# Two transformer layers with cross-attention: the first norm ahead of the context work, the last store in four parts, and a first score with another wait

## The reference

```
x = x + attention(layer_norm(x), layer_norm(x))     # 16 heads of 64, 1024 keys
x = x + attention(layer_norm(x), context)           # 16 heads of 64, 77 keys
x = x + (a * gelu(gate)) @ w2 + b2                  # a, gate = split(layer_norm(x) @ w1 + b1), 1024 wide
```

## Time and profile before

| | us |
|---|---|
| median of 3 runs | 2322.5 |
| lowest and highest | 2322.38, 2325.73 |
| profiled execution, its own time | 2328.06 |
| its span, first to last instruction | 2326.3 |
| TensorE busy | 2142.8 (92%) |
| VectorE busy | 1743.6 (75%) |
| ScalarE busy | 1476.1 (63%) |
| GpSimd busy | 1155.2 (50%) |
| mean granted TensorE clock | 0.990 |

### The profile page before, as it was taken

How to read it: one execution, slowest core, us unless ns; L and a number is a source line. 1 busy time by engine, 2 the same in 40 slices (tenths; PEclk the granted TensorE clock), 3 DMA queues, 4 the chain that set the end, 5 groups by cost and what they waited for, 6 DMA issues and landing times.

```text
span 2326.3 us, 59157 instructions
## 1 busy us (share of the span) xinstructions
PE 2142.8 (92%) x25392; PEld 1434.0 (62%) x25392; DVE 1743.6 (75%) x3148; ACT 1476.1 (63%) x1948; POOL 1155.2 (50%) x730
## 2 busy tenths in 40 slices
PE   4999999999899999989989999998998999999899
PEld 1566666675556666667556666666755666667675
DVE  5888888557588888755768888866576888886664
ACT  2788788345388888823547887773353888786342
POOL 3666665233076766622326766652223667664231
PEclk8999999999999999999999999999999999999999
DMA  3222221000132222001032222100103223210000
GB/s 107 71 73 52 61 62 38 10 31 23 51 105 52 58 74 63 18 10 38 24 83 73 52 75 77 43 27 1 38 23 81 70 61 83 61 36 20 10 11 19
DMA packets 60165, 114.19 MB, mean 49 GB/s; under 512 B 9344, under 2 KB 21632, under 8 KB 59904
## 3 DMA queue, kind: packets, MB, share of 16 engines
q1 hardware_dynamic: 59904, 110.41, 17.5%
HBM read 55.72 MB, written 4.19 MB: 26 GB/s over the span
## 4 chain that ended last, share of the span: by engine, by line
PE 65%; DVE 21%; ACT 9%; issue 3%; DMA 1%; POOL 1%; SPq 0%; POOLq 0%; DVEq 0%; ACTq 0%
PE scores L861 7%; DVE minima L1411 7%; PE scores L854 7%; PE work L831 7%; PE scores L746 6%; PE scores L748 6%; PE scores L747 6%; DVE prob L1426 4%; PE work L746 4%; PE work L747 4%; PE work L748 4%; PE work L883 3%; PE work L879 3%; PE work L881 3%; ACT prob L1214 3%
## 5 line engine op out<-in xcount | busy, mean ns | idle before, releaser
L693 POOL TENSOR_TENSOR prob<-prob 128x1024 f16<-128x1024 f32 x256 | 584.7, 2284 | 556.0 <-ACT prob L1215 545.2
L1411 DVE TENSOR_REDUCE minima<-work 128x1 f32<-128x512 f32 x1024 | 680.2, 684 | 43.0 <-PE work L831 29.4
L1214 ACT ACTIVATE prob<-scores 128x1024 f32<-128x1024 f32 x512 | 525.6, 1026 | 129.2 <-PE scores L861 112.0
L1215 ACT ACTIVATE prob<-scores 128x1024 f16<-128x1024 f32 x512 | 523.3, 1022 | 0.0
L883 PE MATMUL work<-vals,prob 128*128 128x65 f16 x4096 | 429.6, 196 | 0.0
L881 PE MATMUL work<-vals,prob 128*128 128x64 f16 x4096 | 429.4, 193 | 0.0
L879 PE MATMUL work<-vals,prob 128*128 128x65 f16 x4096 | 429.0, 193 | 0.4
L879 PEld LDWEIGHTS work<-vals,prob 128*128 128x128 f16 x4096 | 383.1, 99 | 62.1 <-issue 3.1
L881 PEld LDWEIGHTS work<-vals,prob 128*128 128x128 f16 x4096 | 379.9, 97 | 58.2
L831 PE MATMUL work<-ka,qa 128*128 128x512 f16 x1024 | 390.5, 386 | 24.0 <-DVE minima L1411 18.2
L883 PEld LDWEIGHTS work<-vals,prob 128*128 128x128 f16 x4096 | 380.3, 97 | 0.0
(11 more groups left out here) (160 smaller groups left out, 4179.0 us busy)
## 6 DMA issues: line engine op xcount, KB each, us to landing
qa<-staged_q SPq DMA_DIRECT2D x128, 128.0 KB, 2.3
ka<-staged_k SPq DMA_DIRECT2D x128, 128.0 KB, 2.3
raw_even<-in_pairs SPq DMA_DIRECT2D x32, 384.0 KB, 3.3
raw_odd<-in_pairs SPq DMA_DIRECT2D x32, 384.0 KB, 3.3
raw_odd<-in_pieces SPq DMA_DIRECT2D x20, 512.0 KB, 3.7
raw_even<-in_pieces SPq DMA_DIRECT2D x20, 512.0 KB, 3.6
qb<-staged_q SPq DMA_DIRECT2D x64, 128.0 KB, 2.3
kb<-staged_k SPq DMA_DIRECT2D x64, 128.0 KB, 2.3
```

Source lines behind the costliest of these rows:

```text
L693: pool.tensor_tensor(prob[1][:, slot, :], prob32[:, slot, :], prob[0][:, slot, :], ALU.subtract).then_inc(a.polished, 1)
L1214: act.activation(prob32[:, n % RING, :], source, ACT.Exp)
L1215: act.activation(prob[0][:, n % RING, :], source, ACT.Exp)\
L1411: dve.tensor_reduce(minima[:, t, h:h + 1], out[:, :], AX.X, ALU.max, negate=True)\
```

## The change

The first norm and the six first projections now stand ahead of all work on the context, the ones and the weights on each engine. GpSimd computes its four rstd pairs before it splits the two weight pairs. VectorE sets its first ones and zeros, waits for the constants and starts the norm; the rest of its setting, the context's subtraction and the mask stand behind the mark "v1". ScalarE copies the context behind "v1", and TensorE waits for ones and context there. The context is loaded into `o_nat` in place of `t32`, which the norm uses. The last round's x is stored in four parts, each when its two tiles are done. The first score of a round waits for the round's first six projections alone, not for the seventh.

```diff
--- before.py
+++ after.py
@@ -407,7 +407,7 @@
         x_rows = qa[0]
         spread32 = prob32[:, 0, 0:X_HALF]
         mask_full = prob32[:, 1, 0:len(X_PARTS)]
-        c32 = t32[:, :, :, :].rearrange("p a b c -> p (a b c)")[:, 0:BATCH * 2 * CTX_COLS]
+        c32 = o_nat[:, :, :, :].rearrange("p a b c -> p (a b c)")[:, 0:BATCH * 2 * CTX_COLS]
 
         def o_part(s, t):
 
@@ -588,8 +588,13 @@
                     if (g + 1) % BATCH == 0:
                         sp.wait_ge(bias_added, (g + 1) * 3 + CREDIT)
                         load_rows((g + 1) // BATCH)
-            store(ROUNDS - 1)
-            sp.wait_ge(x_stored, ROUNDS * 16 + CREDIT)
+            for p in range(GROUPS):
+
+                sp.wait_ge(y_free, (ROUNDS * 3 - 1) * TILES + 2 * (p + 1) + 2)
+                tiles = slice(2 * p, 2 * (p + 1))
+                sp.dma_start(io["out"][(ROUNDS - 1) % BATCH, 2 * p * P:2 * (p + 1) * P, :]
+                             .rearrange("(t p) d -> p t d", p=P), x[:, tiles, :]).then_inc(x_stored, 16)
+            sp.wait_ge(x_stored, (ROUNDS - 1 + GROUPS) * 16 + CREDIT)
 
         @block.gpsimd
         def _(pool):
@@ -715,11 +720,11 @@
                     elif n == 6:
                         split_piece(9)
 
-            split_pair("S")
-            split_pair("C")
             pool.sem_inc(bias_added, CREDIT)
             for p in range(GROUPS):
                 norm(0, p)
+            split_pair("S")
+            split_pair("C")
             for g in range(ROUNDS):
                 attention(g)
                 for p in range(GROUPS):
@@ -840,7 +845,7 @@
                     elif step.kind == "score":
                         if pace.here("score") == 0:
 
-                            pe.wait_ge(a.work_free, pace.n(*HIGH) + HIGH_RING)
+                            pe.wait_ge(a.work_free, g * HIGHS + len(first_high) + HIGH_RING)
                         elif pace.here("score") == 1 and g:
 
                             pe.wait_ge(y_free, g * (3 * TILES) + 2)
@@ -1139,11 +1144,12 @@
                             ahead(name)
 
             pe.wait_ge(consts_ready, 10 + 2 * len(X_PARTS))
-            pe.wait_ge(ones_ready, 2)
-            hold(pe, ctx_split, 1)
             for p in range(GROUPS):
                 turn(0, p)
             walk = attention(0)
+            walk("v1")
+            pe.wait_ge(ones_ready, 2)
+            hold(pe, ctx_split, 1)
             for g in range(ROUNDS):
                 cross(g, walk)
                 walk = attention(g + 1) if g + 1 < ROUNDS else None
@@ -1296,17 +1302,18 @@
                     norm(index + 1, 2)
                     norm(index + 1, 3)
 
-            act.wait_ge(ctx_loaded, 16)
+            act.wait_ge(consts_ready, 10 + 2 * len(X_PARTS))
+            act.wait_ge(params_loaded, 16)
+            for p in range(GROUPS):
+                norm(0, p)
+            walk = attention(0)
+            walk("v1")
+            hold(act, ctx_loaded, 16)
             for b in range(BATCH):
                 for part in range(2):
                     cols = slice((2 * b + part) * CTX_COLS, (2 * b + part + 1) * CTX_COLS)
                     act.activation(cT[b][0][:, part, :], c32[:, cols], ACT.Copy).then_inc(ctx_high, 1)
             hold(act, ctx_split, 1)
-            act.wait_ge(consts_ready, 10 + 2 * len(X_PARTS))
-            act.wait_ge(params_loaded, 16)
-            for p in range(GROUPS):
-                norm(0, p)
-            walk = attention(0)
             for g in range(ROUNDS):
                 walk()
                 for p in range(GROUPS):
@@ -1326,21 +1333,6 @@
                     dve.memset(t[p][1][0:DH, :], 0.0)
                 dve.memset(vals[p][:, :, :, 2 * DH:VW], 1.0)
                 dve.memset(kd[p][:, :], 0.0)
-            dve.drain().then_inc(ones_ready, 1)
-            dve.wait_ge(ones_ready, 1)
-            for p in range(2):
-                dve.memset(kb[p][1][0:1, :], 1.0)
-            dve.wait_ge(ctx_high, 2 * BATCH)
-            for b in range(BATCH):
-                high, low = [t[:, :, :].rearrange("p c n -> p (c n)") for t in cT[b]]
-                last = dve.tensor_tensor(low, c32[:, 2 * b * CTX_COLS:2 * (b + 1) * CTX_COLS], high, ALU.subtract)
-            last.then_inc(ctx_split, 1)
-            dve.wait_ge(consts_ready, 10 + 2 * len(X_PARTS))
-            for half in range(2):
-                dve.tensor_scalar(xv[:, half * len(X_PARTS):(half + 1) * len(X_PARTS), 2 * DH], mask[:, :],
-                                  W_SCALE, None, ALU.mult)
-            dve.drain().then_inc(ones_ready, 1)
-            dve.wait_ge(ones_ready, 2)
             dve.sem_inc(y_free, 2)
             dve.sem_inc(inner_ready, 2)
             dve.sem_inc(a.peak_free, PEAK_RING)
@@ -1648,6 +1640,7 @@
                         for name in marks.get(t, []):
                             ahead(name)
 
+            dve.wait_ge(consts_ready, 10 + 2 * len(X_PARTS))
             hold(dve, next_loaded, 16)
             for p in range(GROUPS + 2):
                 if p < GROUPS:
@@ -1658,6 +1651,22 @@
                     split(0, p - 2)
             hold(dve, params_loaded, 16)
             walk = attention(0)
+            walk("v1")
+
+            dve.drain().then_inc(ones_ready, 1)
+            dve.wait_ge(ones_ready, 1)
+            for p in range(2):
+                dve.memset(kb[p][1][0:1, :], 1.0)
+            hold(dve, ctx_high, 2 * BATCH)
+            for b in range(BATCH):
+                high, low = [t[:, :, :].rearrange("p c n -> p (c n)") for t in cT[b]]
+                last = dve.tensor_tensor(low, c32[:, 2 * b * CTX_COLS:2 * (b + 1) * CTX_COLS], high, ALU.subtract)
+            last.then_inc(ctx_split, 1)
+            for half in range(2):
+                dve.tensor_scalar(xv[:, half * len(X_PARTS):(half + 1) * len(X_PARTS), 2 * DH], mask[:, :],
+                                  W_SCALE, None, ALU.mult)
+            dve.drain().then_inc(ones_ready, 1)
+            dve.wait_ge(ones_ready, 2)
             for g in range(ROUNDS):
                 cross(g, walk)
                 walk = attention(g + 1) if g + 1 < ROUNDS else None
```

## The result

The changed kernel takes 2312.4 us (median of five runs, 2310.6 to 2315.0), the kernel before 2324.5 (2322.4 to 2327.4). The ratio is 0.9947, with a 95% interval of 0.9935 to 0.9958: 12.1 us less, between 9.8 and 15.1. The forecast was 9.8 less, and a time of 2312.7. The profiled execution took 2314.0, its span is 2312.2 against 2326.3, so this pair of profiles is 14.1 us apart. It has to be read with care, as will be seen: 5.8 of these 14.1 us came through the granted clock, and over all executions profiled this share was about half of that.

What follows compares the result with a forecast made beforehand. Most of the span was taken as steady state with TensorE and VectorE nearly full, untouched by the diff. Start 3.0, first score 3.9, clock 1.2 and store 1.7 sum to 9.8 us: 2312.7 us, range 2308.5 to 2319.5.

Steps and rivals of the forecast that it cites:

- Start: Norm ahead of context, ones and splits: 4.1 - 0.8 - 0.3 = 3.0 us gained, bounds 0.6 and 5.0.
- The rest of the norm chain: After the first normalise at the start: shifts whole, GpSimd's last power ending at 17.1 instead of 23.31 us.
- the split: GpSimd's first weight split, after the norm: 3.6 us plus 0.25, so the first projection starts at 20.95 instead of 25.05.
- The loss to the clock: TensorE's first projections, after a new 2 us idle: full speed may come later, 0.8 us lost, at worst 2.8.
- The block's overrun: VectorE's moved context and mask work outlasts SyncE's copies before the first maximum by 0.1 to 0.65 us; 0.3 taken.
- First score: Each round's first score no longer waits for the seventh projection: 1.5 + 0.5 + 0.5 + 1.4 = 3.9 us, bounds 1.5 and 4.1.
- Clock: Round 0 on TensorE: without the 1.5 us hole the rise to 2.4 GHz comes earlier; 1.2 us taken, between nothing and 3.3.
- Last store: End of the kernel: the last part is 256 KB instead of 1024; gain 1.7 us, bounds 1.1 and 2.1.
- The estimate by streaming: Last store's landing: about 350 GB/s leaves 0.75 + 1.4 us, against 4.4 before.
- The fourth rival: Granted clock: moved starting points fall into more low clock; about 20 us more at 1.2 GHz cancels the gain; chance 0.05.
- load and drain of 2.66 us: ScalarE's exponential table by the skill's rule: no first-score gain in rounds 1 and 2; the table rival has chance 0.13.
- VectorE and GpSimd block each other: First split beside the last normalise and one subtract: by the rule up to 1.4 us later; 0.4 lies inside the bounds.

Runs made afterwards that it cites:

- early load: Changed kernel plus a small early ScalarE copy to a scratch tile, so its first table load runs near 1 us; 2309.6 us, a second time 2312.5.
- the filling in the kernel before: Kernel before plus unread matmuls in round 0, 24 ahead of the first maximum and one behind each of sixteen maxima; ratio 0.9985.
- three parts timed alone: Kernel before with only the norm moved ahead, only the first score's new wait, or only the four-part last store; ratios 0.9992, 0.9979, 0.9994.
- warm_order: Changed kernel with the first activation table loaded early and GpSimd's first weight split ahead of its fourth rstd pair; 2311.6 us.

## Why the prediction was right, point by point

**The time.** 2312.7 forecast and 2312.4 measured is closer than the working deserves. The gain was 12.1 and not 9.8, and the kernel before took 2324.5 beside it, 2.0 above the 2322.5 that the forecast started from. The two differences cancel, which is luck.

**Start, 3.0 forecast, 2.8 measured.** The first maximum stands at 37.33, 37.07 and 37.70 in the three traces with the new start, no early load and no filling, and at 39.99, 40.52 and 39.94 in three with the old one; at the first shift row the means are 2.7 apart. Right in sum by errors on both sides. The step that was wrong is "The rest of the norm chain ... with nothing foreign in it": ScalarE's table load came into it, 1.27 us. Against it stands the split: 3.6 and another 0.25 had been allowed, and with its drain it took 3.5. So the first projection gained 3.2, not 4.1. The loss to the clock was taken at 0.8; 3.8 us of half speed instead of 2.1 are about 0.9. Its worst case was set too low: 24 matmuls, not 18, lead up to the second k block's end, so 4.1 us and not 2.8. The block's overrun, taken at 0.3, was nothing, and the copies, without the pair that took 2.17 us, gave 0.5 back.

**First score, 3.9, of which 3.05 are fixed.** Round 0 was given 1.5 and has 1.40 at full clock; rounds 1 and 2 have the whole 0.56. Round 3 was given 1.4 and has 0.55 at full clock, since the table load fills the rest there as in round 2. The larger number belonged to the low clock in the one execution that I read.

**Clock, 1.2, measured 2.9 to 3.5 in four rounds.** The term was meant for round 0 alone. There the average without filling is 0.8 (27.38, 24.33 and 24.42 above their floor of 22.72, against the six without the hole above theirs of 21.32). The other 2.7 lie in rounds 1 to 3, 2.0 of them in second heads, where the prediction looked for nothing. Only the 0.85 too much in round 3's first score stood for some of it. That low clock costs this time is shown by the filling in the kernel before. That the hole makes it likelier is shown by the counts above; why is not. First score and clock together were 5.1 in the forecast and 5.9 in the traces.

**Last store, 1.7, measured 2.3.** Right mechanism; the landing was mis-sized, and 2.3 lies outside the bounds of 1.1 to 2.1. The term was to be the mean of 4.4 - 2.8 = 1.6 and of 4.4 - 0.75 - 1.4 = 2.25, which is 1.9, not 1.7; the sum would have been 10.0. The 2.8 lay between a copy within the chip's memory and a load, and the landing took 2.1. The estimate by streaming (2.15) was the better one: no run shows its 350 GB/s as such, but 768 KB more took 2.3 us longer, which is about 340.

**What stays open.** Start 2.7 (at the shift row), first scores and clock 5.9 and store 2.3 make 10.9. The whole measured 12.1, between 9.8 and 15.1. The three parts timed alone make 8.2 (1.9, 4.9, 1.4), each with an interval of some 2.5 us to a side that holds its number from the traces. The kernel before had medians of 2323.0 (34 runs), 2324.4 and 2326.3 at different times. So nothing asks for the parts to strengthen one another, and nothing excludes it. The fourth rival, more low clock with the new starting points, did not come: the four starts lose less than before. What makes the clock fall is open.

**Two rules weighed.** Of the Trainium skill's load and drain of 2.66 us (ScalarE: Activation LUTs, What ACT_TABLE_LOAD costs): the trace has the load's 1.28 and 0.02 behind it; the measurement decides. That VectorE and GpSimd block each other (the Trainium skill, SBUF — State Buffer, Who interferes with whom): the trace agrees more than I gave it; the normalise took 1.74 against 0.73 beside the split, and in warm_order such delays, 1.6 us of them, outweighed the gain.

## What to carry to other kernels

In these traces an activation table is loaded in front of the first activation, behind that activation's wait: whoever moves or removes the first activation of an engine that starts idle should give it a small early one in its place. Where a first stretch of TensorE work is cut by a hole, ask not only what the hole costs but whether the clock comes up ahead of it; and read that from several executions, since one may be off by several us, and from the stretch behind as well, where a third of the first scores' gain lay here. A floor read in one round holds for another only if the same instructions stand there: round 0, without the table load, gained 1.40 where the others gained 0.55. Work put into an idle stretch has to stand ahead of the wait that ends the stretch, in the engine's own queue.

## What was not expected of the hardware

The two kernels' first projection matmuls took 0.43 us from start to start, though a window there gives the granted clock as 1.00. Later the windows agree with the durations. So the value given before the clock's first change in these traces is not to be trusted, and the durations decide. Filling TensorE's idle time with unread matmuls kept the clock at 2.4 GHz through 16 maxima, and those ran at 0.60 us each instead of 0.69, though VectorE paces them: at the low clock TensorE had been in their way too. And with TensorE busy without a break the clock still fell for some us in one head, which no run here explains.
